# Cross attention and feed-forward on one core: output bias prepared early on 32 rows, weight splits in eight pieces

## The chip, the cores and the metric

One core of one Trainium2 chip runs the kernel in one launch. The metric is the time of an execution on the device in microseconds; several runs are made and their median is compared.

## The reference

x has 16 x 100 = 1600 tokens of 512, the context 16 x 361 = 5776 keys of 512. Sixteen heads of 32 dimensions attend from all tokens to all keys; queries, keys, values and probabilities are rounded to 8 bits. A feed-forward part with 1408 hidden channels follows.

```python
q = (x @ Wq + bq) ; k, v = split(cond @ Wkv + bkv)        # x is layernormed
q, k, v = fq_sym(q * scale), fq_sym(k), fq_sym(v)          # 127 steps, by row / by channel
attn = fq_unsigned(softmax(q @ k.T))                       # 255 steps
x = x + (attn @ v) @ Wp + bp
x13 = quant(layernorm(x)) @ w13.T ; x1, x3 = split(x13)
x = x + quant(rmsnorm(relu(x1) ** 2 * x3) * norm_w) @ w2.T
```

## The kernel before

**Stages.** The program is written out engine by engine, each with its own instruction list and semaphores. First comes *group 0*: keys and values of heads 0 to 3 are computed from 46 blocks of 128 keys (a block is a *unit*, the last has 16 keys; four units are a *batch*, so 12 batches), and between batches the queries of a token tile. For each unit TensorE does four f32 products for the keys (L580), one bf16 product for the key bias (L587) and four f32 products for the values (L582); each f32 product is two passes in the profile. Then comes the main loop over 200 *steps*, `for i in range(NA)`. A step is one tile of 128 tokens of one head against all 5776 keys, in four chunks of 1536 (the last 1168):

- TensorE: scores of the chunk (L640), attention times values of the step four before (L659), and one slice of a unit of the next group (groups 1 to 3) or, from step 160 on, pieces of the output projection (`rows_turn`, `rows_product`).
- VectorE: evicts the chunk from PSUM and takes its minimum (L1120), then the row's minimum (L1142). Between the chunks it takes maxima of the key and value batches.
- ScalarE: one exp over the whole row into bytes (L947), so one L947 a step; it also evicts units.
- SP: issues all transfers in one queue, in order. One transpose of the bytes a step (L524) goes ahead when the exp is done and GpSimd has emptied the buffer (two buffers).
- GpSimd (POOL): unpacks the bytes in four casts a step (`unpack`, L1369), and does key parts, value rounding and the odd jobs. Its order is a list `todo` of (key, work) that is sorted by key; a key is a step with a fraction, and `unpack(i, part)` stands at `i + 2.3 + 0.2 * part`.

Thirteen tiles of the feed-forward part end the program.

**What the change touches.** A bias is added on TensorE as a product of ones with a tile that has the bias in three bf16 parts (high, middle, low), one part in each of rows 0, 1, 2, and zeros below. `BK3` is that tile for the keys; VectorE builds it at the start (s_b3). The product in `unit` contracts over all 128 rows of `ones` and `BK3`. When the last unit is done, the same tile is written again for the output bias (`BP3 = BK3`), by GpSimd in five parts, `bias_parts`, at keys 154.15 to 158.15, from bp that SP loads at step 153 (`BP_AT`) into a buffer of the output rows. `rows_product` reads it (L690) after semaphore r_b3.

`split_w13(k)` splits block k of the feed-forward weight (128 x 2816) into a rounded part and a rest that TensorE reads later. Block 0 is loaded at steps 158 to 161 and split at key 163, block 1 loaded at 177 to 180 and split at key 182. Blocks 2 and 3 are done by other engines at the end.

The two lines that set this order:

```python
todo += [(WP_AT + 8.15 + part, bias_parts, (part,)) for part in range(5)]          # WP_AT = 146
todo += [(step + WSP + 1, split_w13, (k,)) for k, step in EARLY_W.items() if k < 2] # WSP = 4
```

Of the kernel before, what the change touches and what calls it, by code (L numbers as in the profile page):

```python
# [35 lines left out]
ALU = mybir.AluOpType  # L36
# [41 lines left out]
WP_AT = (NG - 1) * PHASE - 4  # L78
BP_AT = WP_AT + 7
EARLY_W = {0: (NG - 1) * PHASE + 8, 1: NA - PAIRT + 2, 2: NA - PAIRT + 10}  # L80
# [3 lines left out]
ROWS_AT = [(NG - 1) * PHASE + 10 + 3 * t for t in range(NT)]  # L84
GSPLIT = 640
W2_SPLIT = [(0, 4), (4, 8), (8, NF)]
RING = 4
# [54 lines left out]
def build(nc, x, ctxt, ctxl, Wq, bq, Wkv, bkv, Wp, bp, w13T, w2T, norm_w, eye, Qd, Kd, Od, Rd, out):  # L142
    ctx = ExitStack()
    with ctx:
# [51 lines left out]
        with ExitStack() as early:  # L196
            BK = tmp("BK", [C], F32, early)
            BR = tmp("BR", [C], F32, early)
            BH = tmp("BH", [C], BF16, early)
            BM = tmp("BM", [C], BF16, early)  # L200
            BL = tmp("BL", [C], BF16, early)
            BQ = tmp("BQ", [C], F32, early)
        S = ring("S", 2, [KP], F32)
        Pr = ring("Pr", 2, [NU // 2, P, 2], U8)
# [16 lines left out]
        with ExitStack() as early:  # L221
# [3 lines left out]
            OT = tmp("OT", [NK - 1, P], F32, early)  # L225
        BP, BPT = XO[0], XO[1].bitcast(BF16)[:, 0:C]
        BP3 = BK3[:, :]
        XIF = [tmp("XIF0", [NK, P], F32R)]
# [33 lines left out]
        def halves(k):  # L262
# [10 lines left out]
                   s_nrm s_nr0 s_un s_ao0 s_ao1 s_dve s_act s_pool   # L273
                   r_ol0 r_ol1 r_x0 r_x1 r_b r_b3 r_tp r_ot r_pr r_xo r_st0 r_st1
                   f_tp f_tpe f_pr f_x1 f_xb0 f_xb1 f_sd1 f_sd1d f_xi f_xit
# [48 lines left out]
        def _(sp):  # L324
# [79 lines left out]
            for g in range(NG):  # L404
                sp.dma_start(BV[:, g:g + 1], bkv[C + g * GC:C + (g + 1) * GC].rearrange("(p a) -> p a", a=1)).then_inc(M["s_bv"], 16)
            load_x(2)
            nxt = RING
            for b in range(NBT):
                if b >= 3:
                    store_k(0, b - 3)  # L410
                while nxt < min(NU, NB * b + 7):
                    load_unit(0, nxt)
                    nxt += 1
                for t in Q_AFTER[b][:1]:
                    if 3 <= t + 3 < NT:
# [71 lines left out]
            for i in range(NA):  # L487
# [15 lines left out]
                if 0 <= i - WP_AT < NK:  # L503
                    k = i - WP_AT
                    sp.dma_start(WP[:, k, :], Wp[k * P:(k + 1) * P, :]).then_inc(M["f_c"], 16)
                if i == BP_AT:
                    sp.wait_ge(M["s_vg"], (NG - 1) * NBT)
                    sp.dma_start(BP, bp.partition_broadcast(P)).then_inc(M["r_b"], 16)
                for k, first in EARLY_W.items():
# [53 lines left out]
        def _(pe):  # L563
            def unit(g, u, slices=range(NK)):
# [12 lines left out]
                for c in slices:  # L577
# [6 lines left out]
                    if c == 1:  # L584
                        if k == 0:
                            pe.wait_ge(M["s_b3"], 1)
                        pe.matmul(bank[0:n, 0:GC], ones[:, 0:n], BK3[:, g * GC:(g + 1) * GC], start=False, stop=True)  # L587
                if NK - 1 in slices:
# [84 lines left out]
            def rows_product(t, piece):  # L673
# [11 lines left out]
                if piece == NK - 1:  # L685
                    if t == 0:
                        pe.wait_ge(M["r_b3"], 1)
                    pe.wait_ge(M[f"r_x{t % 2}"], 16 * (t // 2 + 1))
                pe.matmul(PK[0:n, cols], ident[0:n, 0:n], XR[t % 2][0:n, cols], start=False, stop=False)
                last = pe.matmul(PK[0:n, cols], ones[:, 0:n], BP3[:, cols], start=False, stop=True)  # L690
                if piece == 2 * NK - 1:
# [308 lines left out]
        def _(v):  # L1000
# [262 lines left out]
        def _(gp):  # L1263
# [32 lines left out]
            def v_quant(g, b):  # L1296
# [10 lines left out]
                gp.tensor_scalar(VB[k % VRING][:, 0:w], q, 1.0, -MAGIC, ALU.mult, ALU.add).then_inc(M["s_vg"], 1)  # L1307

            def scale_wp(k):

                gp.wait_ge(M["f_c"], 16 * NK)
                gp.wait_ge(M["s_vr"], NG)
                gp.tensor_scalar(WP[:, k, :], WP[:, k, :], SV[:, k:k + 1], 1.0, ALU.mult, ALU.mult).then_inc(M["s_wp"], 1)

            def bias_parts(part):

                if part == 0:
                    gp.wait_ge(M["r_b"], 16)
                    gp.wait_ge(M["s_ku"], NG * NU)
                    link(gp.tensor_scalar(BP3, BP, 1.0, 0.0, ALU.mult, ALU.add))  # L1320
                    link(gp.tensor_tensor(BP, BP, BP3, ALU.subtract))
                elif part == 1:
                    link(gp.tensor_scalar(BP3, BP3, ident[:, 0:1], 1.0, ALU.mult, ALU.mult))
                    link(gp.tensor_scalar(BPT, BP, 1.0, 0.0, ALU.mult, ALU.add))
                elif part == 2:
                    link(gp.tensor_tensor(BP, BP, BPT, ALU.subtract))
                    link(gp.tensor_scalar(BPT, BPT, ident[:, 1:2], 1.0, ALU.mult, ALU.mult))
                elif part == 3:
                    link(gp.tensor_tensor(BP3, BP3, BPT, ALU.add))
                    link(gp.tensor_scalar(BPT, BP, ident[:, 2:3], 1.0, ALU.mult, ALU.mult))  # L1330
                else:
                    gp.tensor_tensor(BP3, BP3, BPT, ALU.add).then_inc(M["r_b3"], 1)

# [37 lines left out]

            def split_w13(k):

                high, low, full = halves(k)
                gp.wait_ge(M[f"f_w{k % 2}"], 16 * WSP * (k // 2 + 1))
                gp.tensor_scalar(high, full, 1.0, 0.0, ALU.mult, ALU.add).then_inc(M["f_hi"], 1)
                gp.wait_ge(M["f_hi"], k + 1)
                gp.tensor_tensor(low, full, high.bitcast(F32), ALU.subtract).then_inc(M["f_lo"], 1)

            gp.wait_ge(M["cst"], 1)  # L1380
            for b in range(NBT + 1):
                if b < NBT:
                    k_scale(0, b)
                if b:
                    k_parts(0, b - 1)
            for a in range(VRING):
                link(gp.memset(VB[a], 0.0))
# [8 lines left out]
            todo += [(WP_AT + 6.15 + k, scale_wp, (k,)) for k in range(NK)]  # L1396
            todo += [(WP_AT + 8.15 + part, bias_parts, (part,)) for part in range(5)]
            todo += [(i + 2.3 + 0.2 * part, unpack, (i, part)) for i in range(NA) for part in range(NPV)]
            todo += [(PAIRT * (p + 1) + LAG + 1, normalise, (p,)) for p in range(H // 2 - 1)]
            todo += [(step + WSP + 1, split_w13, (k,)) for k, step in EARLY_W.items() if k < 2]  # L1400
            todo += [(NA - PAIRT + FULL + FRONT + LAG + 0.15, normalise_front, ())]
# [59 lines left out]
```

## Time and profile before

| | |
|---|---|
| runs | 1914.78, 1923.21, 1927.03 us; median 1923.21 |
| profiled execution | 1914.62 us, span 1912.7 us |
| TensorE (PE) | 1661.8 us busy, 87% |
| VectorE (DVE) | 1696.9 us busy, 89% |
| ScalarE (ACT) | 1372.0 us busy, 72% |
| GpSimd (POOL) | 1447.2 us busy, 76% |
| group 0 | from the start to about 180 us |
| main loop | from about 175 us to about 1670 us |

The span is the time from the first to the last instruction in the trace; the execution's own time has 1.9 us more around it. The profiled execution is at the low end of the runs. Busy shares are averages over stages with different limits. A wait in brackets behind a row is idle time of that engine just before the row, and what ended it.

### The profile page before, as it was taken

The page shows a single profiled execution, that of the slowest core. Times are in us where ns is not written, and L with a number is a line of the kernel's source. Part 1 is how long each engine was busy: PE and PEld are TensorE (multiplying, and loading weights), DVE is VectorE, ACT ScalarE, POOL GpSimd, SP SyncE. Part 2 cuts the span into 40 slices and gives each one's busy share as a digit, 9 for nine tenths or more (in the row PEclk, how much of TensorE's full clock was granted, in tenths as well). Part 3 has the DMA queues.
Part 4 walks back from the last instruction along what each step waited for, and adds up shares of the span by engine and source line. Part 5 has one row for each costly group of instructions (what it writes and reads, how often), then busy time and mean ns, then how long its engine had stood idle before and what let it go on. Part 6 is the DMA issues. An engine that isn't in the chain of part 4 may idle for free.

```text
span 1912.7 us, 40494 instructions
## 1 busy us (share of the span) xinstructions
PE 1661.8 (87%) x16216; PEld 1129.8 (59%) x16216; DVE 1696.9 (89%) x2665; ACT 1372.0 (72%) x1324; POOL 1447.2 (76%) x1166
## 2 busy tenths in 40 slices
PE   7997888888888888889888888898878888679998
PEld 6884666665556665655556665544445555368876
DVE  6766999999999999999999999999889999976665
ACT  2444888898779898888888888887778878632322
POOL 1341798999998888989988888899988898832332
PEclk9998999997799999977999999755689999889999
DMA  5666989997999899969997998888878988732221
GB/s 177 212 199 172 188 175 179 189 181 144 202 182 189 168 182 185 186 134 202 178 202 152 179 190 167 159 159 148 181 150 165 200 167 158 157 107 51 65 56 45
DMA packets 851482, 309.87 MB, mean 162 GB/s; under 512 B 784928, under 2 KB 813920, under 8 KB 851168
## 3 DMA queue, kind: packets, MB, share of 16 engines
q1 hardware_dynamic: 851296, 307.29, 77.9%
q8 instruction: 129, 2.11, 0.5%
q14 instruction: 57, 0.47, 0.1%
HBM read 74.25 MB, written 39.58 MB: 60 GB/s over the span
## 4 chain that ended last, share of the span: by engine, by line
DVE 36%; PE 23%; POOL 15%; issue 13%; DMA 6%; ACT 5%; SPq 2%; POOLq 0%; DVEq 0%; ACTq 0%
DVE S L1120 32%; POOL PT L1369 11%; PE PS L744 5%; DMA PP<-Pr 4%; PE PS L640 4%; PE PK L580 3%; PE PK L795 3%; PE PS L607 2%; ACT Pr L947 2%; PE PO L659 1%; PE PK L582 1%; POOL VV L1304 1%; PE PO L582 1%; PE PO L580 1%; DVE kam L1034 1%
## 5 line engine op out<-in xcount | busy, mean ns | idle before, releaser
L1120 DVE TENSOR_SCALAR_CACHE_REDUCE S<-PS,SQN 128x1536 f32<-128x1536 f32 (+1 forms) x768 | 1286.8, 1714 | 65.3 <-PE PS L640 56.7
L947 ACT ACTIVATE Pr<-S,MS 128x5888 uint8<-128x5888 f32 x200 | 1041.5, 5207 | 216.1 <-DVE MJ L1142 155.1
L1369 POOL CAST PT<-PP 128x1536 uint16<-128x1536 uint8 (+1 forms) x800 | 1102.4, 1423 | 82.7 <-DMA PP<-Pr 82.0
L640 PE MATMUL PS<-KT,QT 96*128 96x512 bf16 (+1 forms) x2496 | 719.0, 413 | 130.4 <-DVE S L1120 117.9
L659 PEld LDWEIGHTS PO<-VI,PT 128*128 128x128 f16 x9200 | 350.0, 99 | 307.4 <-issue 150.9
L659 PE MATMUL PO<-VI,PT 128*128 128x32 bf16 x9200 | 366.2, 180 | 72.2 <-ACT AO L905 58.7
L640 PEld LDWEIGHTS PS<-KT,QT 96*128 96x128 bf16 (+1 forms) x2496 | 209.0, 104 | 342.4 <-issue 166.6
L580 PE MATMUL PK<-WG,CT 128*128 128x128 f32 (+1 forms) x1272 | 220.6, 303 | 13.1 <-DMA CT<-ctxt 8.1
L582 PE MATMUL PK<-CT,WG 128*128 128x128 f32 (+1 forms) x1272 | 212.7, 295 | 0.0
L580 PEld LDWEIGHTS PK<-WG,CT 128*128 128x128 f32 (+1 forms) x1272 | 172.9, 199 | 16.4 <-issue 11.8
L582 PEld LDWEIGHTS PK<-CT,WG 128*128 128x128 f32 x1272 | 167.0, 194 | 1.8 <-issue 0.6
L744 PE MATMUL PS<-W,XIF 128*128 128x512 f32 (+3 forms) x624 | 144.4, 389 | 10.0 <-issue 6.5
L1272 POOL TENSOR_TENSOR KB<-KB,kam 128x512 f32<-128x512 f32 (+1 forms) x48 | 48.7, 1015 | 130.7 <-DVE kam L1041 130.7
L744 PEld LDWEIGHTS PS<-W,XIF 128*128 128x128 f32 (+1 forms) x624 | 115.1, 190 | 40.0 <-POOL XIF L1412 8.9
L1284 POOL TENSOR_TENSOR KD<-KE,kam 128x512 f32<-128x512 f32 (+1 forms) x48 | 48.6, 1013 | 63.0 <-ACT KE L832 63.0
L819 ACT ACTIVATE KB<-PK 128x128 f32<-128x128 f32 (+1 forms) x159 | 42.8, 269 | 65.5 <-PE PK L582 65.2
L1207 DVE SCALAR_TENSOR_TENSOR G<-PS,sc,TG 128x1408 f32<-128x1408 f32 (+1 forms) x13 | 21.9, 1683 | 58.3 <-PE PS L744 58.3
L992 ACT ACTIVATE TG<-G 128x1408 f32<-128x1408 f32 (+1 forms) x13 | 18.0, 1384 | 77.1 <-DVE G L1207 77.1
L1423 POOL TENSOR_SCALAR GW<-GW,sc 128x1408 f32<-128x1408 f32 (+1 forms) x13 | 18.6, 1434 | 71.2 <-DVE sc L1228 71.2
L795 PE MATMUL PK<-W,IQF 128*128 128x512 f32 (+1 forms) x286 | 68.3, 394 | 4.2 <-POOL IQF L1418 1.8
L1120 DVE DVE_READ_ACCUMULATOR S<-PS,SQN 128x1 f32 x768 | 63.9, 83 | 0.0
L795 PEld LDWEIGHTS PK<-W,IQF 128*128 128x128 f32 (+1 forms) x286 | 51.6, 184 | 19.3 <-issue 5.3
(155 smaller groups left out, 1455.3 us busy)
## 6 DMA issues: line engine op xcount, KB each, us to landing
CT<-ctxt SPq DMA_DIRECT2D x180, 256.0 KB, 3.3
k_rows<-KS SPq DMA_DIRECT2D x44, 512.0 KB, 4.2
q_rows<-QS SPq DMA_DIRECT2D x13, 512.0 KB, 4.2
W13F<-w13T SPq DMA_DIRECT2D x12, 352.0 KB, 3.6
PP<-Pr SPq DMA_TRANSPOSE x200, 5.9
XT<-x SPq DMA_DIRECT2D x12, 256.0 KB, 3.3
XR<-x SPq DMA_DIRECT2D x12, 256.0 KB, 3.3
base_rows<-XO SPq DMA_DIRECT2D x12, 256.0 KB, 3.4
```

The lines of the kernel that those rows point to most:

```text
L580: pe.matmul(bank[0:n, 0:GC], CT[k % RING][:, d, 0:n], WG[:, d, 0, :], start=(d == 0), stop=False)
L582: last = pe.matmul(bank[:, GC:GC + n], WG[:, d, 1, :], CT[k % RING][:, d, 0:n], start=(d == 0), stop=(d == NK - 1))
L640: last = pe.matmul(PS[n % 2][p0:p0 + r, f:f + w], QT[h % 3][0:PARTS * HD, q0:q0 + r], KT[h % 3][0:PARTS * HD, c * CHUNK + f:c * CHUNK + f ...
L659: last = pe.matmul(PO[:, 0:w], PT[i % 2][:, u, :].bitcast(F16), VI[g % 2][:, u, h * HD:h * HD + w], start=(u == 0), stop=(u == NU - 1))
L744: last = pe.matmul(PS[half][0:n, f:f + w], XF[:, c, 0:n], W13[:, c, a, half * FF + f:half * FF + f + w], start=(c == 0 and a == 0), stop=( ...
L795: last = pe.matmul(PK[0:n, :], IQF[t % 2][:, k, 0:n], W2[:, k, a, :], start=(k == 0 and a == 0), stop=(k == NF - 1 and a == WPARTS - 1))
L819: act.activation(KB[kb % 2][0:n, u % NB, :, 0:HD], bank[0:n, 0:GC].rearrange("p (h d) -> p h d", d=HD), ACT.Copy)
L947: act.activation(Pr[i % 2].rearrange("p t q b -> p t b q"), S[i % 2].rearrange("p (t b q) -> p t b q", b=2, q=P), ACT.Exp, bias=MS[:, i % ...
L1120: v.tensor_scalar(S[i % 2][:, c * CHUNK:c * CHUNK + CW[c]], PS[n % 2][:, 0:CW[c]], neg_step, None, ALU.mult, ALU.min, accum_out=MN[:, i % ...
L1272: gp.tensor_tensor(KA, KA, kam[:, kb % 2, 1, 0:m].unsqueeze(2).to_broadcast([P, m, HD]), ALU.mult).then_inc(M["s_kn"], 1)
L1284: gp.tensor_tensor(v3(KD), v3(KE), kam[:, kb % 2, 0, 0:m].unsqueeze(2).to_broadcast([P, m, HD]), ALU.mult).then_inc(M["s_k6"], 1)
L1369: gp.tensor_copy(PT[i % 2][:, 2 * t0:2 * t1, :].rearrange("p (t b) q -> p t b q", b=2), PP[i % 2][:, t0:t1, :].bitcast(U8).rearrange("p t ...
```

## The change

1. `bias_parts` goes. `bias_part(part)` takes bp apart into three bf16 tiles `BPP[0..2]` in full, in batches 2, 3 and 4 of group 0 (two vector operations, two, one). bp is loaded once by SP ahead of the loads of unit 4.
2. In batch 6 of group 0, SP moves one row of each of the three tiles into rows 32, 33, 34 of `BK3`. VectorE waits for these three transfers before the main loop.
3. The key bias products contract over rows 0 to 31 (`KEY_ROWS`), the output bias products over rows 32 to 63 (`OUT_ROWS`).
4. `split_w13(k)` becomes eight pieces of 352 columns, each at a key of its own, one step apart: 163 to 170 and 182 to 189.

```diff
-BP_AT = WP_AT + 7
+WPIECES = 8
+BIAS_AT = 2
+KEY_ROWS, OUT_ROWS = slice(0, 32), slice(32, 64)
...
-        BP, BPT = XO[0], XO[1].bitcast(BF16)[:, 0:C]
-        BP3 = BK3[:, :]
+        BP3 = BK3[OUT_ROWS, :]
...
             load_x(2)
+            sp.dma_start(BP, bp.partition_broadcast(P)).then_inc(M["r_b"], 16)
...
+                if b == BIAS_AT + PARTS + 1:
+                    sp.wait_ge(M["r_bp"], PARTS)
+                    sp.wait_ge(M["s_b3"], 1)
+                    for part in range(PARTS):
+                        row = OUT_ROWS.start + part
+                        sp.dma_start(BK3[row:row + 1, :], BPP[part][row:row + 1, :]).then_inc(M["r_b3"], 16)
...
-                if i == BP_AT:
-                    sp.wait_ge(M["s_vg"], (NG - 1) * NBT)
-                    sp.dma_start(BP, bp.partition_broadcast(P)).then_inc(M["r_b"], 16)
...
-                        pe.matmul(bank[0:n, 0:GC], ones[:, 0:n], BK3[:, g * GC:(g + 1) * GC], start=False, stop=True)
+                        pe.matmul(bank[0:n, 0:GC], ones[KEY_ROWS, 0:n], BK3[KEY_ROWS, g * GC:(g + 1) * GC], start=False, stop=True)
...
-                        pe.wait_ge(M["r_b3"], 1)
+                        pe.wait_ge(M["r_b3"], 16 * PARTS)
...
-                last = pe.matmul(PK[0:n, cols], ones[:, 0:n], BP3[:, cols], start=False, stop=True)
+                last = pe.matmul(PK[0:n, cols], ones[OUT_ROWS, 0:n], BP3[:, cols], start=False, stop=True)
...
+            v.wait_ge(M["r_b3"], 16 * PARTS)
             for i in range(NA):
...
+            def bias_part(part):
+
+                if part == 0:
+                    gp.wait_ge(M["r_b"], 16)
+                gp.tensor_scalar(BPP[part], BP, 1.0, 0.0, ALU.mult, ALU.add).then_inc(M["r_bp"], 1)
+                if part < PARTS - 1:
+                    gp.wait_ge(M["r_bp"], part + 1)
+                    link(gp.tensor_tensor(BP, BP, BPP[part], ALU.subtract))
...
-            def split_w13(k):
-
-                high, low, full = halves(k)
+            def split_w13(k, e):
+
+                cols = slice(e * 2 * FF // WPIECES, (e + 1) * 2 * FF // WPIECES)
+                high, low, full = [half[:, cols] for half in halves(k)]
                 gp.wait_ge(M[f"f_w{k % 2}"], 16 * WSP * (k // 2 + 1))
...
+                if e < WPIECES - 1:
+                    link(gp.tensor_scalar(high, full, 1.0, 0.0, ALU.mult, ALU.add))
+                    link(gp.tensor_tensor(low, full, high.bitcast(F32), ALU.subtract))
+                else:
...
-            todo += [(WP_AT + 8.15 + part, bias_parts, (part,)) for part in range(5)]
...
-            todo += [(step + WSP + 1, split_w13, (k,)) for k, step in EARLY_W.items() if k < 2]
+            todo += [(step + WSP + 1 + e, split_w13, (k, e)) for k, step in EARLY_W.items() if k < 2
+                     for e in range(WPIECES)]
```

GpSimd in the main loop, around keys 154 to 156 of the kernel before. BK is the bias tile, XO a buffer that holds bp there, the CASTs unpack one step.

```order
L1320 TENSOR_SCALAR BK<-XO 128x512 [waits s_ku,r_b]
L1321 TENSOR_TENSOR XO<-XO,BK 128x512 [waits s_pool]
L1369 CAST PT<-PP 128x1536 [waits s_pvp,s_tr0,s_pool]
L1369 CAST PT<-PP 128x1536 [waits s_pvp] x2
L1369 CAST PT<-PP 128x1280 [waits s_pv]
L1344 TENSOR_TENSOR AO<-AO,RZ 128x12x32 [waits s_rz,s_pve]
L1344 TENSOR_TENSOR AO<-AO,RZ 128x12x32 [waits s_pool]
L1347 TENSOR_TENSOR AO<-AO,RZ 128x64 [waits s_pool]
L1313 TENSOR_SCALAR WP<-WP,SV 128x512 [waits s_vr,f_c]
L1323 TENSOR_SCALAR BK<-BK,ident 128x512
L1324 TENSOR_SCALAR XO<-XO 128x512 [waits s_pool]
```

The rows of L1320 to L1332 are gone there. Their successors stand in group 0, between the key parts of one batch and the key scale of the next (line numbers of the changed kernel):

```order
L1301 TENSOR_TENSOR KS<-KE 128x16x32 [waits s_kd,s_k8]
L1321 TENSOR_SCALAR BPP<-BP 128x512 [waits r_b]
L1324 TENSOR_TENSOR BP<-BP,BPP 128x512 [waits r_bp]
L1280 TENSOR_TENSOR KB<-KB,kam 128x16x32 [waits s_kr,s_pool]
L1292 TENSOR_TENSOR KD<-KE,kam 128x512 [waits s_kh,s_kc]
L1295 TENSOR_TENSOR KE<-KD 128x512 [waits s_k6]
L1301 TENSOR_TENSOR KS<-KE 128x16x32 [waits s_kd,s_k8]
L1321 TENSOR_SCALAR BPP<-BP 128x512
L1324 TENSOR_TENSOR BP<-BP,BPP 128x512 [waits r_bp]
```

The nine operations with a wait for the load became five, each pair ahead of a scale that waits for VectorE.

SP's queue in group 0 of the changed kernel, at batch 6:

```order
L366 DMA XT<-x 128x512 [waits s_xn]
L426 DMA BK<-BPP 1x16x32 [waits s_b3,r_bp]
L426 DMA BK<-BPP 1x16x32 x2
L395 DMA q_rows<-QS 128x2048 [waits s_qs]
L341 DMA k_rows<-KS 128x4x512 [waits s_kh,s_kp]
L333 DMA CT<-ctxt 128x512 [waits s_ku] x4
```

The row transfers stand between a load of x and a store of query rows; the loads of the next units (CT) come behind.

GpSimd at the split of block 0, before:

```order
L1376 TENSOR_SCALAR W<-W13F 128x2816 [waits f_w0]
L1378 TENSOR_TENSOR W<-W13F,W 128x2816 [waits f_hi]
L1369 CAST PT<-PP 128x1536 [waits s_pvp,s_tr1]
L1369 CAST PT<-PP 128x1536 [waits s_pvp] x2
L1369 CAST PT<-PP 128x1280 [waits s_pv]
```

and now:

```order
L1376 TENSOR_SCALAR W<-W13F 128x352 [waits f_w0]
L1377 TENSOR_TENSOR W<-W13F,W 128x352 [waits s_pool]
L1367 CAST PT<-PP 128x1536 [waits s_pvp,s_tr1,s_pool]
L1367 CAST PT<-PP 128x1536 [waits s_pvp] x2
L1367 CAST PT<-PP 128x1280 [waits s_pv]
L1376 TENSOR_SCALAR W<-W13F 128x352 [waits f_w0]
L1377 TENSOR_TENSOR W<-W13F,W 128x352 [waits s_pool]
L1367 CAST PT<-PP 128x1536 [waits s_pvp,s_tr0,s_pool]
L1367 CAST PT<-PP 128x1536 [waits s_pvp] x2
L1367 CAST PT<-PP 128x1280 [waits s_pv]
L1376 TENSOR_SCALAR W<-W13F 128x352 [waits f_w0]
```

One long pair became eight short ones with the four casts of a step between each two.

## Rows read from the trace of the kernel before

**Rows 1.** Windows: us, busy us (and instructions) of each engine, TensorE clock, DMA share, GB/s.
```profile
50.00:100.00 50.00, 50.00 (x360) 41.94 (x359) 38.52 (x71) 21.54 (x61) 20.11 (x20) 1.00 0.65 203
```
**Rows 2.** Timeline of ScalarE, the exp of each step: start us, us, idle before.
```profile
1328.95 5.21 ACT L947 ACTIVATE Pr<-S,MS 128x5888 uint8<-128x5888 f32 x1 [1.74 <-DVE MJ L1142]
1335.98 5.21 ACT L947 ACTIVATE Pr<-S,MS 128x5888 uint8<-128x5888 f32 x1 [1.61 <-DVE MJ L1142]
...
1354.05 5.21 ACT L947 ACTIVATE Pr<-S,MS 128x5888 uint8<-128x5888 f32 x1 [4.59 <-DMA PP<-Pr]
...
1382.75 5.21 ACT L947 ACTIVATE Pr<-S,MS 128x5888 uint8<-128x5888 f32 x1 [1.66 <-DVE MJ L1142]
```
**Rows 3.** Timeline of GpSimd at the first part of the bias.
```profile
1328.49 0.70 POOL L1313 TENSOR_SCALAR WP<-WP,SV 128x512 f32<-128x512 f32 x1
1330.72 0.62 POOL L1320 TENSOR_SCALAR BK<-XO 128x512 bf16<-128x512 f32 x1 [1.53 <-DMA XO<-bp]
1331.42 1.16 POOL L1321 TENSOR_TENSOR XO<-XO,BK 128x512 f32<-128x512 f32 x1
1332.64 5.48 POOL L1369 CAST PT<-PP 128x1536 uint16<-128x1536 uint8 x4
```
**Rows 4.** Timeline of GpSimd at the split of block 0.
```profile
1394.08 2.54 POOL L1376 TENSOR_SCALAR W<-W13F 128x2816 fp32r<-128x2816 f32 x1
1396.71 6.18 POOL L1378 TENSOR_TENSOR W<-W13F,W 128x2816 fp32r<-128x2816 f32 x1
1402.84 10.91 POOL L1369 CAST PT<-PP 128x1536 uint16<-128x1536 uint8 x8
```
**Rows 5.** Timeline of ScalarE, exps around the splits of blocks 0 and 1.
```profile
1396.34 5.21 ACT L947 ACTIVATE Pr<-S,MS 128x5888 uint8<-128x5888 f32 x1 [1.04 <-DVE MJ L1142]
...
1415.54 5.21 ACT L947 ACTIVATE Pr<-S,MS 128x5888 uint8<-128x5888 f32 x1 [5.74 <-DMA PP<-Pr]
...
1430.03 5.21 ACT L947 ACTIVATE Pr<-S,MS 128x5888 uint8<-128x5888 f32 x1 [1.66 <-DVE MJ L1142]
...
1443.63 5.21 ACT L947 ACTIVATE Pr<-S,MS 128x5888 uint8<-128x5888 f32 x1 [1.04 <-DVE MJ L1142]
...
1464.53 5.21 ACT L947 ACTIVATE Pr<-S,MS 128x5888 uint8<-128x5888 f32 x1 [1.04 <-DVE MJ L1142]
...
1535.67 5.21 ACT L947 ACTIVATE Pr<-S,MS 128x5888 uint8<-128x5888 f32 x1 [1.66 <-DVE MJ L1142]
...
1572.34 5.21 ACT L947 ACTIVATE Pr<-S,MS 128x5888 uint8<-128x5888 f32 x1 [1.48 <-DVE MJ L1142]
1579.13 5.21 ACT L947 ACTIVATE Pr<-S,MS 128x5888 uint8<-128x5888 f32 x1 [1.42 <-DVE MJ L1142]
```
**Rows 6.** Timeline of GpSimd in group 0.
```profile
72.07 1.05 POOL L1272 TENSOR_TENSOR KB<-KB,kam 128x512 f32<-128x512 f32 x1 [7.16 <-DVE kam L1041]
```
**Rows 7.** Timeline of TensorE, last units of group 0; 128*16 is rows*columns of the array.
```profile
134.53 0.22 PE L587 MATMUL PO<-BK,ones 128*128 128x128 bf16 x1
134.58 1.11 PE L582 MATMUL PO<-CT,WG 128*128 128x128 f32 x8
135.53 1.06 PE L580 MATMUL PK<-WG,CT 128*128 128x128 f32 x8
...
136.48 1.11 PE L582 MATMUL PK<-CT,WG 128*128 128x128 f32 x8
137.52 1.05 PE L580 MATMUL PO<-WG,CT 128*16 128x128 f32 x8
138.40 0.22 PE L587 MATMUL PO<-BK,ones 128*16 128x128 bf16 x1
138.55 1.06 PE L582 MATMUL PO<-CT,WG 128*128 128x16 f32 x8
```
**Rows 8.** Timeline of TensorE, the bias of a unit of group 1 and what follows.
```profile
351.06 0.22 PE L587 MATMUL PK<-BK,ones 128*128 128x128 bf16 x1
351.56 0.82 PE L640 MATMUL PS<-KT,QT 96*128 96x512 bf16 x3 [0.28 <-DVE S L1120]
```

More of the change, by code:

```diff
@@ L202, in build @@
             BQ = tmp("BQ", [C], F32, early)
+            BP = tmp("BP", [C], F32, early)
+            BPP = ring("BPP", PARTS, [C], BF16, early)
         S = ring("S", 2, [KP], F32)
@@ L273, in build @@
                    s_nrm s_nr0 s_un s_ao0 s_ao1 s_dve s_act s_pool
-                   r_ol0 r_ol1 r_x0 r_x1 r_b r_b3 r_tp r_ot r_pr r_xo r_st0 r_st1
+                   r_ol0 r_ol1 r_x0 r_x1 r_b r_bp r_b3 r_tp r_ot r_pr r_xo r_st0 r_st1
                    f_tp f_tpe f_pr f_x1 f_xb0 f_xb1 f_sd1 f_sd1d f_xi f_xit
@@ L1313, in scale_wp @@
                 gp.tensor_scalar(WP[:, k, :], WP[:, k, :], SV[:, k:k + 1], 1.0, ALU.mult, ALU.mult).then_inc(M["s_wp"], 1)
[L1315 to L1332, printed above, removed]
             def normalise(p):
@@ L1370, in unpack @@
                                PP[i % 2][:, t0:t1, :].bitcast(U8).rearrange("p t (q b) -> p t b q", b=2)).then_inc(M["s_un"], 1)
-            def split_w13(k):
-                high, low, full = halves(k)
+            def split_w13(k, e):
+                cols = slice(e * 2 * FF // WPIECES, (e + 1) * 2 * FF // WPIECES)
+                high, low, full = [half[:, cols] for half in halves(k)]
                 gp.wait_ge(M[f"f_w{k % 2}"], 16 * WSP * (k // 2 + 1))
-                gp.tensor_scalar(high, full, 1.0, 0.0, ALU.mult, ALU.add).then_inc(M["f_hi"], 1)
-                gp.wait_ge(M["f_hi"], k + 1)
-                gp.tensor_tensor(low, full, high.bitcast(F32), ALU.subtract).then_inc(M["f_lo"], 1)
+                if e < WPIECES - 1:
+                    link(gp.tensor_scalar(high, full, 1.0, 0.0, ALU.mult, ALU.add))
+                    link(gp.tensor_tensor(low, full, high.bitcast(F32), ALU.subtract))
+                else:
+                    gp.tensor_scalar(high, full, 1.0, 0.0, ALU.mult, ALU.add).then_inc(M["f_hi"], 1)
+                    gp.wait_ge(M["f_hi"], k + 1)
+                    gp.tensor_tensor(low, full, high.bitcast(F32), ALU.subtract).then_inc(M["f_lo"], 1)
             gp.wait_ge(M["cst"], 1)
@@ L1385, in _ @@
                     k_parts(0, b - 1)
+                if 0 <= b - BIAS_AT < PARTS:
+                    bias_part(b - BIAS_AT)
             for a in range(VRING):
```

## The prediction

> **What bounds the kernel now.** I read the page first, then the windows, then the timeline of ScalarE, whose big exp (L947) marks one step of the main loop each time, then GpSimd and TensorE in the stretches that the diff touches. The page shows VectorE and TensorE both busy for over 85% of the span, and its chain of waits gives VectorE's evictions (L1120) the largest share. Three stretches matter here.
>
> The first is group 0, the key and value product ahead of the loop: TensorE is busy 50.00 of 50 us there [rows 1]. What is added to it costs time one for one.
>
> The second is the loop where the bias is taken apart. A step takes 7.03 us when nothing disturbs it (1328.95 to 1335.98), but 1328.95 to 1382.75 holds seven steps in 53.80 us, and the exp at 1354.05 stood 4.59 us for the transpose of an earlier step [rows 2]. That transpose waits until GpSimd has emptied its buffer, and GpSimd was at the bias: 1.53 us of waiting for the transfer of bp, then vector work between the casts [rows 3]. The loss is 53.80 - 7 x 7.03 = 4.6 us.
>
> The third are the two splits of a weight block. GpSimd holds 2.54 + 6.18 us in one piece, 8.76 us from 1394.08 to the next cast at 1402.84 [rows 4]. The exp at 1415.54 then waits 5.74 us for the transpose. 1396.34 to 1430.03 holds four steps in 33.69 us; three steps from 1443.63 to 1464.53 take 20.90, so 6.97 each, and the loss is 33.69 - 27.9 = 5.8 us. For block 1, 1535.67 to 1572.34 holds five steps in 36.67 us; the step behind takes 6.79, so the loss is 36.67 - 33.95 = 2.7 us [rows 5]. Together 13.1 us lie in these three places. Between them the pace is set by VectorE and TensorE, and the change does nothing to that.
>
> **The change part by part.** *Bias out of the loop.* The nine vector operations and the wait go. GpSimd gives up 3.5 us at the first part alone (the bias casts stand between 1328.49 + 0.70 and 1332.64) and has four parts more to do, each ahead of a cast. What is late next is the step itself at 7.03 us. Weight loads of block 0 lie in the same steps and go on lengthening the transposes; I leave 0.4 us for them. Gain 4.2 us, between 2.5 and 4.6.
>
> *Bias ahead of the loop.* Three tensor_scalar of 0.62 and two tensor_tensor of 1.16 us [rows 3] come to 4.2 us, spread over batches 2, 3 and 4 of group 0, where GpSimd stands idle 7.16 us before each key scale [rows 6]. Cost 0. If that cover were gone it would be at most 4.2 us. The load of bp is one more issue on SP ahead of unit 4, and the three row transfers (1 KB each) stand in SP's queue ahead of a store of query rows and the key store; both their waits are met by work done long before. Behind them stand the loads of four units. I take 0; it could be 1 us, if those loads come late. VectorE's new wait ahead of the loop is met more than 50 us earlier. Nothing is queued behind it but the loop that starts later anyway.
>
> *Splits in eight pieces.* A tensor_scalar of 352 columns: 0.62 at 512, 2.54 at 2816, so 0.83 ns a column and 0.49 us. A tensor_tensor: 1.16 and 6.18, 2.18 ns a column, 0.81 us. Gaps behind linked operations are 0.08 and 0.06 us [rows 3, 4]. A piece costs 1.44 us, eight 11.5 instead of 8.8, but a step then asks 5.48 + 1.44 = 6.92 us of GpSimd, once a step. Against 6.97 that fits; I leave 0.6 us of the 5.8 for jitter: gain 5.2, between 2 and 5.8. Against 6.79 it is 0.13 too long for eight steps, 1.0 us, and 0.4 for late transposes: gain 1.3, between -1 and 2.7. The weights are needed only at the end of the loop, so their later finish costs nothing. The three gains are 10.7 us.
>
> *Bias products on 32 rows.* This is the part that the title of the change hardly names. Each of the 184 key bias products (L587) and the 26 output bias products (L690) now contracts over 32 partitions instead of 128, so TensorE goes from a matmul on all rows to one on 32 and back. No row has that shape. The nearest is the last unit of a group, with 16 columns of the array [rows 7]: L582 runs 0.95 us to the next matmul on the full array (134.58 to 135.53), but 1.04 when the next has 16 columns (136.48 to 137.52), and from the bias to L582 it is 0.05 us ordinarily (134.53 to 134.58), 0.15 on the way back to the full array (138.40 to 138.55). So 0.09 in and 0.10 out, 0.19 us per bias product. In group 0 TensorE is the bound and 44 of the 46 units stand on the path (waits stand between the last two and the loop): 44 x 0.19 = 8.4 us. In groups 1 to 3, 138 units would make 26 us if all were exposed, but there TensorE waits 0.28 us for VectorE right behind the bias [rows 8], which covers 0.19; I take 1.1 us. The 26 output products make 4.9 us if exposed; they stand in the loop too, and I take 0.5. Ends of the price: below, -0.05 us, the time that a bias product takes between its neighbours, if on its own rows it ran beside them; above, 0.38, twice what the rows show. I take the value of the rows, the nearest that there are.
>
> The Trainium skill has a rule that speaks against this part: "TensorEngine Tiling", section "Key Properties", says that a change of tiling mode, other than a change of tile, drains the engine. By that rule the trace agrees, with 0.09 and 0.10 us at [rows 7]; the page gives no figure.
>
> **The sum.** -4.2 - 5.2 - 1.3 + 8.4 + 1.1 + 0.5 = -0.7 us. The profiled execution took 1914.62 us (span 1912.7 and 1.9 around it), so 1913.9 for its like. It was at the low end of the runs; their median is 1923.21, 0.45% above. From the median: 1922.5 us. A difference under about 1%, 19 us, can't be told from none on this kernel. So the change should come out as no change: what GpSimd gives back in the loop, TensorE pays in group 0.
>
> **The rivals.**
> *The switch to 32 rows is free.* For it: the matmul that the rows show is narrow in columns, the new ones in rows, and no row has those. Against it: the narrow unit pays on the way in and on the way out, so it looks like a change of shape and not like a cost of the columns. It gives 1923.2 - 10.7 = 1912.5 us. The Trainium skill, "TensorE: Matmul & The Clock Gate", section "Why this matters for your kernels", says that a single matmul over 32 rows takes the same time as one over 128; with that alone this rival's time would hold. The matmul's own duration is the 0.22 us of L587 [rows 7], and it is silent on the changes around it.
>
> *The switch costs more, and the kernel is slower.* Place: group 0, where nothing covers TensorE. Price 0.38 us each, 44 x 0.38 = 16.7, with 1.6 in the rest, against 10.7 gained: +7.6, so 1930.8 us. It decides the sign from (10.7 - 1.6) / 44 = 0.21 us each, and my 0.19 is right below. If the 0.28 of cover in groups 1 to 3 is then too short, 138 times 0.1 us come on top, and that is over 1%, 1944 us.
>
> *The pieces fill GpSimd.* 6.92 us a step leaves no room for late transposes. If both splits lose as much as before, only the bias is gained: -4.2 + 10.0 = +5.8, 1929.0 us. Against it: the loop is double buffered, and a piece goes where GpSimd stood waiting for a transpose.
>
> *The bias gain is hidden anyway*, since the quantised values just before had GpSimd late already: 4.2 us less, 1926.7.
>
> **How the numbers follow.** Forecast 0.48; free switch 0.17; dearer switch 0.20; full GpSimd 0.08; hidden bias gain 0.07. All but the worst of the dearer switch lie within 1% of 1923.2. Faster by over 1% needs 19 us, more than the 13.1 that lie in all three places: 0.03, for what I don't see. Slower by over 1%: 0.08, a third of the dearer switch and a little. Within 1%: 0.89. The range reaches from all 13.1 us gained and no price (1910) to the dearer switch with half the gains lost (+13, 1936), a microsecond wider on each side for the runs' own spread.
>
> **What would show it.** Right: in group 0 the step from bias to L582 at about 0.15 us instead of 0.05, a unit at about 2.09 instead of 1.90 (134.58 to 136.48, [rows 7]), and the first exp of the loop some 8 us later. In the loop no exp waits over 3 us for a transpose near the old 1354 and 1415; GpSimd shows pairs of about 0.5 and 0.8 us between casts. In groups 1 to 3 TensorE's waits for VectorE shrink, and the steps keep their length. Wrong: a unit in group 0 still at 1.90 (free switch) or over 2.2 us (dearer); longer steps in groups 1 to 3; in the split stretches steps of 7.2 us and more with GpSimd never idle.

## The result, and the profile after

The changed kernel takes 1926.08 us (median of 22 runs) where the kernel before takes 1920.90 beside it: ratio 1.0031, interval 1.0016 to 1.0045, so 3 to 9 us slower. A second set of runs gave 1.0039 (1.0017 to 1.0061). The forecast of no change, -0.7 us, was too low: GpSimd's gains came and TensorE and the rest gave back more. The experiments found that one part of the change alone, the splits in pieces, is faster than both kernels: 0.9929 to 0.9955 in three sets of runs. One run of all that follow, of pieces_third, took 2387.88 us at a mean granted clock of 0.552; it is counted among that kernel's 11 runs and left out of every ratio and fit.

The profiled execution of the changed kernel took 1919.13 us. The page, busy time of the engines:

```profile
PE 1686.4 (88%) x16216; PEld 1136.5 (59%) x16216; DVE 1697.6 (89%) x2665; ACT 1373.1 (72%) x1324; POOL 1452.4 (76%) x1190
```

TensorE has the same 16216 instructions as before and is busy 24.6 us longer; VectorE and ScalarE stand within 1.1 us of before, GpSimd has 5.2 us more for its 24 more instructions. The chain of waits, by engine and by line:

```profile
DVE 37%; PE 25%; issue 14%; POOL 10%; DMA 7%; ACT 5%; SPq 3%; POOLq 0%; DVEq 0%; ACTq 0%
DVE S L1128 33%; POOL PT L1367 7%; PE PS L751 5%; PE PS L647 5%; DMA PP<-Pr 4%; PE PK L587 3%; PE PK L802 3%; ACT Pr L954 2%; PE PS L614 2%; PE PK L589 2%; PE PO L666 2%; PE PO L589 1%; PE PK L689 1%; PE PO L587 1%; SPq L531 1%
```

GpSimd has 10% of the chain, 15% before; TensorE 25%, 23% before. Group 0 shows one place where TensorE is busy longer. Timeline of TensorE in the changed kernel, the units that answer to [rows 7]; L594 is the bias product, L589 the values, L587 the keys:

```profile
134.78 0.23 PE L594 MATMUL PO<-BK,ones 32*128 32x128 bf16 x1
134.93 1.16 PE L589 MATMUL PO<-CT,WG 128*128 128x128 f32 x8
135.93 1.06 PE L587 MATMUL PK<-WG,CT 128*128 128x128 f32 x8
136.91 0.22 PE L594 MATMUL PK<-BK,ones 32*128 32x128 bf16 x1
137.07 1.16 PE L589 MATMUL PK<-CT,WG 128*128 128x128 f32 x8
```

The kernel before, between the keys at 135.53 and the values at 136.48 of [rows 7]:

```profile
136.42 0.22 PE L587 MATMUL PK<-BK,ones 128*128 128x128 bf16 x1
```

The product itself takes 0.22 us as before. Around it: 0.15 to the values (0.05 before), 0.98 from the keys to it (0.89 before), and 1.00 over the values (0.95 before). A unit takes 137.07 - 134.93 = 2.14 us instead of 1.90.

Timeline of ScalarE in the changed kernel, exps where the bias was taken apart [rows 2], and at the split of block 0 [rows 5]:

```profile
1355.77 5.21 ACT L954 ACTIVATE Pr<-S,MS 128x5888 uint8<-128x5888 f32 x1 [1.61 <-DVE MJ L1150]
1362.79 5.21 ACT L954 ACTIVATE Pr<-S,MS 128x5888 uint8<-128x5888 f32 x1 [1.61 <-DVE MJ L1150]
1369.80 5.21 ACT L954 ACTIVATE Pr<-S,MS 128x5888 uint8<-128x5888 f32 x1 [1.61 <-DVE MJ L1150]
...
1404.58 5.21 ACT L954 ACTIVATE Pr<-S,MS 128x5888 uint8<-128x5888 f32 x1 [1.03 <-DVE MJ L1150]
1413.12 5.21 ACT L954 ACTIVATE Pr<-S,MS 128x5888 uint8<-128x5888 f32 x1 [1.66 <-DVE MJ L1150]
...
1434.02 5.21 ACT L954 ACTIVATE Pr<-S,MS 128x5888 uint8<-128x5888 f32 x1 [1.66 <-DVE MJ L1150]
```

Both stalls for the transpose, 4.59 and 5.74 us before, are gone: the exps wait for VectorE (MJ) alone. Timeline of GpSimd between two steps there [rows 4]:

```profile
1402.03 0.49 POOL L1376 TENSOR_SCALAR W<-W13F 128x352 fp32r<-128x352 f32 x1
1402.60 0.93 POOL L1377 TENSOR_TENSOR W<-W13F,W 128x352 fp32r<-128x352 f32 x1
1403.59 5.49 POOL L1367 CAST PT<-PP 128x1536 uint16<-128x1536 uint8 x4
1409.06 0.49 POOL L1376 TENSOR_SCALAR W<-W13F 128x352 fp32r<-128x352 f32 x1
```

GpSimd never rests here and takes 7.03 us for a step (1402.03 to 1409.06). Three steps from 1413.12 take 20.90, 6.97 each: the two paces almost meet.

### The profile page after: what moved, and what is told of

The parts are those of the page before. It is cut to its first block, busy times and chain, and to the rows that moved or that the text cites. A ratio compares the mean times of both kernels' runs of the same rounds, so it can differ in the third digit from the quotient of the medians.

```text
span 1917.2 us, 40523 instructions
## 1 busy us (share of the span) xinstructions
PE 1686.4 (88%) x16216; PEld 1136.5 (59%) x16216; DVE 1697.6 (89%) x2665; ACT 1373.1 (72%) x1324; POOL 1452.4 (76%) x1190
## 4 chain that ended last, share of the span: by engine, by line
DVE 37%; PE 25%; issue 14%; POOL 10%; DMA 7%; ACT 5%; SPq 3%; POOLq 0%; DVEq 0%; ACTq 0%
DVE S L1128 33%; POOL PT L1367 7%; PE PS L751 5%; PE PS L647 5%; DMA PP<-Pr 4%; PE PK L587 3%; PE PK L802 3%; ACT Pr L954 2%; PE PS L614 2%; PE PK L589 2%; PE PO L666 2%; PE PO L589 1%; PE PK L689 1%; PE PO L587 1%; SPq L531 1%
## 5 line engine op out<-in xcount | busy, mean ns | idle before, releaser
L647 PEld LDWEIGHTS PS<-KT,QT 96*128 96x128 bf16 (+1 forms) x2496 | 203.7, 104 | 323.7 <-issue 150.8
L587 PE MATMUL PK<-WG,CT 128*128 128x128 f32 (+1 forms) x1272 | 220.2, 303 | 13.3 <-DMA CT<-ctxt 9.0
L589 PE MATMUL PK<-CT,WG 128*128 128x128 f32 (+1 forms) x1272 | 213.4, 295 | 0.0
L587 PEld LDWEIGHTS PK<-WG,CT 128*128 128x128 f32 (+1 forms) x1272 | 172.7, 199 | 16.4 <-issue 12.4
L589 PEld LDWEIGHTS PK<-CT,WG 128*128 128x128 f32 x1272 | 166.2, 193 | 2.8
L689 PE MATMUL PK<-WP,OT 128*128 128x256 f32 (+1 forms) x168 | 62.8, 465 | 0.0
```

The source lines that it names most:

```text
L587: pe.matmul(bank[0:n, 0:GC], CT[k % RING][:, d, 0:n], WG[:, d, 0, :], start=(d == 0), stop=False)
L589: last = pe.matmul(bank[:, GC:GC + n], WG[:, d, 1, :], CT[k % RING][:, d, 0:n], start=(d == 0), stop=(d == NK - 1))
L647: last = pe.matmul(PS[n % 2][p0:p0 + r, f:f + w], QT[h % 3][0:PARTS * HD, q0:q0 + r], KT[h % 3][0:PARTS * HD, c * CHUNK + f:c * CHUNK + f ...
L689: pe.matmul(PK[0:n, cols], OT[:, k, half:half + n], WP[:, k, cols], start=(k == 0 and half == 0), stop=False)
```

## The experiments

There are eighteen measurements: thirteen new kernels, and five repeats. A single profile is a weak witness on this kernel: the kernel before, profiled once more, took 9.9 us longer. So times come from medians, and the profiles serve to read where single steps fall. The ratios are against the kernel before on the same chip; its median in each set is 1918.04, 1919.37, 1921.06, 1917.35 and 1917.94 us.

| kernel | runs | median us | ratio (interval) |
|---|---|---|---|
| narrow_g0 | 6 | 1928.91 | 1.0070 (1.005 to 1.009) |
| narrow_loop | 9 | 1925.51 | 1.0038 (1.0016 to 1.0061) |
| narrow_out | 12 | 1921.18 | 1.0012 (0.9995 to 1.0029) |
| rows96_all | 12 | 1910.06 | 0.9959 (0.9941 to 0.9977) |
| pieces_only | 6 | 1906.29 | 0.9929 (0.9917 to 0.9941) |
| bias_only | 12 | 1921.46 | 1.0006 (0.9986 to 1.0025) |
| rows64, before_again | 1 each | 1936.08, 1924.47 | none: single runs |
| pieces_again | 11 | 1911.21 | 0.9949 (0.9933 to 0.9964) |
| no_bias | 6 | 1907.16 | 0.9937 (0.9916 to 0.9959) |
| early_only | 12 | 1916.20 | 0.9980 (0.9964 to 0.9996) |
| narrow_all | 4 | 1939.01 | 1.0100 (1.0076 to 1.0124) |
| after_again | 12 | 1925.19 | 1.0039 (1.0017 to 1.0061) |
| rows96_again | 12 | 1910.12 | 0.9957 (0.9939 to 0.9976) |
| pieces_rows96 | 8 | 1910.15 | 0.9963 (0.9947 to 0.9979) |
| pieces_third | 11 | 1909.96 | 0.9955 (0.9937 to 0.9974) |
| alloc_only | 8 | 1910.05 | 0.9958 (0.9938 to 0.9979) |
| early_dead | 12 | 1909.81 | 0.9961 (0.9942 to 0.9980) |

Much of the spread between runs of one kernel goes with the mean granted clock of TensorE that each run lists: the correlation is -0.96 over 12 runs of rows96_all, -0.76 over 22 of the changed kernel, and between -0.14 and -0.93 in the other sets of runs of one kernel. I fitted all runs of the five sets together, with a constant for each kernel and each set and one slope for the clock. The slope is -5.8 us for 0.01 more of clock, and the spread (standard deviation) that is left is 3.3 us instead of 4.2. One run of the kernel before has a clock of 0.864, far from all others; without it the slope is -7.8, and the figures below move by 1.1 us at most, each within its own uncertainty. Below, "at equal clock" is a figure of this fit, against the kernel before, with twice its standard error. A change that moved the clock itself would have that part taken out, so the ratios stand beside it.

**The narrow bias products.**

```diff
-pe.matmul(bank[0:n, 0:GC], ones[:, 0:n], BK3[:, g * GC:(g + 1) * GC], ...)
+r = slice(0, 32) if g == 0 else slice(0, P)        # narrow_g0; narrow_loop: if g > 0
+pe.matmul(bank[0:n, 0:GC], ones[r, 0:n], BK3[r, g * GC:(g + 1) * GC], ...)
...
-last = pe.matmul(PK[0:n, cols], ones[:, 0:n], BP3[:, cols], ...)
+last = pe.matmul(PK[0:n, cols], ones[0:32, 0:n], BP3[0:32, cols], ...)   # narrow_out
```

> The kernel before with one edit: the 46 key bias products of group 0 contract over 32 rows, all others over 128 as before. Theory (a change of array shape costs about 0.25 us a bias product, as the changed kernel's units of 2.14 us instead of 1.89 show, and TensorE is the bound in group 0): 44 x 0.25 = 11 us less what a wait of 1.5 us for key context at unit 44 absorbs and what the queries behind it wait anyway, so +7 to +10 us, and the first exp 8 us later. Rival (group 0's loss in the changed kernel came from the load of bp and the row transfers in SP's queue): 0 us.

> The kernel before with one edit: the 138 key bias products of groups 1 to 3 contract over 32 rows. Theory A (TensorE's slack behind a bias does not cover the change of shape in every step: the changed kernel lost 5.0 us between the first exp and step 154, where nothing else was changed): +3 to +7 us. Rival B (the forecast: 0.28 us of slack hides 0.25): 0 to +1 us. Rival C (those 5.0 us are drift between two executions): 0, with the steps' lengths as before.

> The kernel before with one edit: the 26 output bias products contract over 32 rows. Theory (exposed in the third of the steps where the projection runs, since TensorE sets the step there): +2 to +4 us, seen as longer steps every third step from 160 on. Rival (hidden, as forecast): 0 to +0.5 us.

> The kernel before with every bias product, the key's in all four groups and the output's, on 32 rows. The three parts alone measured +13.4, +7.3 and +2.3 us. If the costs add up: +23 us against the kernel before. If they share what the loop can hide: +14 us, which is what the changed kernel is above the same kernel with 96 rows.

At equal clock the four are +12.6 (3.0), +6.3 (2.5), +2.3 (2.3) and, all together, +17.8 (3.5). The first two are clear of zero, the output products alone are not (their ratio's interval is 0.9995 to 1.0029). The parts add up to 21.2, within the uncertainty of 17.8. In groups 1 to 3 the surcharge is visible too. Timeline of TensorE at a unit of narrow_loop, and a like place of before:

```profile
524.92 0.69 PE L580 MATMUL PK<-WG,CT 128*128 128x128 f32 x4
525.55 0.23 PE L588 MATMUL PK<-BK,ones 32*128 32x128 bf16 x1
525.71 0.82 PE L641 MATMUL PS<-KT,QT 96*128 96x512 bf16 x3
```

```profile
506.39 0.69 PE L580 MATMUL PK<-WG,CT 128*128 128x128 f32 x4
506.92 0.22 PE L587 MATMUL PK<-BK,ones 128*128 128x128 bf16 x1
506.98 0.81 PE L640 MATMUL PS<-KT,QT 96*128 96x512 bf16 x3
```

From the keys to the scores it is 0.79 us instead of 0.59: 0.2 more, 138 times, of which 6 us arrive at the end.

**How many rows.** `slice(0, 64)` for all bias products on the kernel before, and on the changed kernel 96 rows for the key, with the output bias in rows 96 to 98 and its products over all 128 rows:

```diff
-KEY_ROWS, OUT_ROWS = slice(0, 32), slice(32, 64)
+KEY_ROWS, OUT_ROWS = slice(0, 96), slice(96, 128)
-last = pe.matmul(PK[0:n, cols], ones[OUT_ROWS, 0:n], BP3[:, cols], ...)
+last = pe.matmul(PK[0:n, cols], oneo[:, 0:n], BP3[:, cols], ...)   # BP3 = BK3[:, :]; oneo: 1 in OUT_ROWS, else 0
```

> The kernel before with key and output bias products over 64 rows. If what is paid is a change of the array's shape, whatever its size, a unit of group 0 takes 2.14 us as with 32 rows. If it grows with the rows left out, about 2.05 us. If only 32 rows are paid for, 1.89 us.

> The changed kernel, but with key bias products over rows 0 to 95, the output bias in rows 96 to 98, and the output bias products over all 128 rows with a stationary tile that is one in rows 96 to 127 and zero above. If the price is that of the array's shape and 96 rows count as the full array (scores have 96 rows), a unit in group 0 is back at 1.89 us and all that GpSimd gives back is kept: -11 to -13 us against the kernel before. Rival (any count of rows other than 128 is paid for): a unit of 2.14 us and +2 to +5 us. Rival (the gain of the pieces is lost elsewhere too): -4 to -8 us.

> The changed kernel with the key products on 96 rows and the output products on 128, once more. Against after_again it has the narrow products taken out and nothing else: 14 to 20 us less (about 0.25 us for each of 211 narrow products, where they are not hidden, is at most 50; group 0 alone is 11).

Timelines of TensorE in group 0, rows64 and then rows96_again:

```profile
133.98 1.16 PE L582 MATMUL PO<-CT,WG 128*128 128x128 f32 x8
134.97 1.06 PE L580 MATMUL PK<-WG,CT 128*128 128x128 f32 x8
135.96 0.23 PE L588 MATMUL PK<-BK,ones 64*128 64x128 bf16 x1
136.12 1.16 PE L582 MATMUL PK<-CT,WG 128*128 128x128 f32 x8
```

```profile
134.51 1.11 PE L590 MATMUL PO<-CT,WG 128*128 128x128 f32 x8
135.46 1.06 PE L588 MATMUL PK<-WG,CT 128*128 128x128 f32 x8
136.35 0.22 PE L595 MATMUL PK<-BK,ones 96*128 96x128 bf16 x1
136.41 1.11 PE L590 MATMUL PK<-CT,WG 128*128 128x128 f32 x8
```

On 64 rows a unit takes 2.14 us as on 32 (133.98 to 136.12), on 96 rows 1.90 as on 128. So the price does not grow with the rows left out: it is there in full at 64 and 32 rows and absent at 96. That 32 and 64 rows make the array change its shape and 96 do not fits this, but is inferred: the rows of the trace name only the rows used (96*128). rows64 is a single execution, of which the unit time is used here. Two sets of runs put the kernel with 96 rows 8 us under before; against after_again it is 14.0 (2.5) us less at equal clock.

> The changed kernel as it is, beside the two runs below on one chip. Its first measurement: ratio 1.0031, some 6 us above the kernel before. The parts alone, added up, give more: narrow products +18 to +20 (narrow_all, narrow_g0 + narrow_loop + narrow_out), the rest of the change -8 (rows96_all), so +10 to +12. If the parts add up, this run should come out nearer 1.005 than 1.003; if they do not, it stays at 1.003 and the splits in pieces take back part of what the narrow products cost.

The changed kernel stayed near its first measurement, +7.4 (2.3) at equal clock. Narrow products 17.8 and the rest -6.6 would make 11; with the uncertainties of both, that can't be told from 7.

**The splits alone, the bias move alone.** pieces_only is the kernel before with `split_w13(k, e)` of the change and nothing else; bias_only is rows96_all with the splits in one piece:

```diff
-            todo += [(step + WSP + 1, split_w13, (k,)) for k, step in EARLY_W.items() if k < 2]
+            todo += [(step + WSP + 1 + e, split_w13, (k, e)) for k, step in EARLY_W.items() if k < 2
+                     for e in range(WPIECES)]
```

> The kernel before with one edit: the two splits in eight pieces each; bias and rows as before. Theory (each split in one piece held GpSimd 8.76 us and cost 5.8 and 2.7 us; the pieces fit the step): -5 to -8 us, no exp near either split waiting over 3 us for a transpose. Rival (6.9 us of GpSimd a step is too much, the loss is spread over eight steps): -2 to +3 us, with steps of 7.2 us and GpSimd never idle.

> The kernel of rows96_all with each split in one piece again, so only the bias is moved, on rows that keep the array's shape. Theory: -3 to -5 us, all of it between steps 154 and 161. Rival (the rounded values just before have GpSimd late anyway, or the early work and the transfers in group 0 cost something): -1 to +2 us. With pieces_only it should add up to rows96_all, -7.9 us.

> The kernel before, unchanged, for a second profile of it. If the 5.0 us that the changed kernel lost between step 0 and step 154 came from its narrow products, this profile has the first one's steps to within 1 us. If they were largely the way that transfers and steps happen to fall, its steps drift from the first one's by several us, above all between steps 42 and 50.

> The kernel before with both splits in eight pieces and nothing else, once more, so that it shares its chip with the two runs beside it. If its first measurement stands (ratio 0.9929), it comes out 12 to 15 us under the kernel before.

The splits in pieces bring -7.3 (1.6) at equal clock over three sets, 9 to 14 us by the ratios. The bias move brings +1.4 (2.4): no gain. Yet its stall is gone. The time between the starts of two exps, counted by steps from the first exp (0), in the twenty profiles:

| steps | what lies there | without the edit | with it |
|---|---|---|---|
| start to 0 | group 0 on 128 or 96 rows; on 32 or 64 | 183.6 to 190.0, mean 186.9 | 194.4 to 196.9, mean 195.4 |
| 154 to 161 | bias in the loop; not | 52.1 to 56.0 | 48.5 to 49.7 |
| 163 to 167 | block 0 in one piece; in eight | 30.8 to 33.7 | 27.2 to 29.5 |
| 181 to 190 | block 1 in one piece; in eight | 65.7 to 69.2 | 61.2 to 64.5 |

No row overlaps. The means differ by +8.5, -5.4, -4.2 and -4.5 us. TensorE's granted clock is not alike in all of them: for block 0 the two profiles of 27.2 us had 1.00. Among profiles with 0.85 to 0.89 it is 32.0 to 33.6 us in one piece and 28.1 to 29.5 in eight, so the gain is not the clock's.

**Where the bias gain goes.** no_bias is pieces_only without any output bias (no load, no operations, and the output products add what the key bias tile holds). early_only is pieces_only with the early bias work of the change on 96 rows added, and the old work kept:

```diff
 # early_only, against pieces_only
+            sp.dma_start(BP, bp.partition_broadcast(P)).then_inc(M["r_b"], 16)    # ahead of unit 4
+                    bias_part(b - BIAS_AT)                                        # GpSimd, group 0
+                        sp.dma_start(BK3[row:row + 1, :], BPP[part][row:row + 1, :]).then_inc(M["r_b3"], 16)
+            v.wait_ge(M["r_b3"], 16 * PARTS)
+                        pe.matmul(bank[0:n, 0:GC], ones[KEY_ROWS, 0:n], BK3[KEY_ROWS, g * GC:(g + 1) * GC], ...)
```

> Splits in eight pieces, and the output bias left out altogether: neither its load nor GpSimd's nine operations run, and the output products read the key bias tile as it stands (the output bias isn't added). It bounds from above what moving the output bias out of the loop can give. Theory A (the move gives 4 us in the loop, and something ahead of the loop or later takes it back): 4 us under pieces_again. Theory B (the stall of the bias steps is made good further on in any case, since the wait behind it is shorter by what it was late): within 1.5 us of pieces_again.

> Splits in eight pieces, the bias work of the changed kernel ahead of the loop (load, GpSimd's parts, three transfers of a row each, key products on 96 rows, VectorE's wait for the rows), and the old bias work in the loop kept as well. It differs from pieces_again by the early work alone. Theory A (the early work costs what the move gives): 4 to 6 us above pieces_again. Theory B (the early work is free, as forecast): within 1.5 us of it.

Theory A (the move gains in the loop, and something else takes it back) has the better of it: against pieces_only and its repeats at equal clock, no_bias is -4.1 (3.1), as the stall of the loop, and early_only is +3.5 (2.5). Both are only just clear of zero. What of the early work costs it?

```diff
 # pieces_rows96, against pieces_only
+                        pe.matmul(bank[0:n, 0:GC], ones[0:96, 0:n], BK3[0:96, g * GC:(g + 1) * GC], ...)
 # alloc_only: tiles for BP, BPP and oneo set aside, unused
+            BE = tmp("BE", [C], F32, early)
+            BPP = ring("BPP", PARTS, [C], BF16, early)
 # early_dead: alloc_only, and
+            sp.dma_start(BE, bp.partition_broadcast(P)).then_inc(M["r_e"], 16)
+                    bias_part(b - BIAS_AT)
```

> Splits in eight pieces and the key bias products on 96 rows instead of 128, no other part of the change. It tells what of the early bias work cost early_only its 5 us against pieces_again. If 96 rows cost something that the unit time of group 0 does not show: 3 to 5 us above pieces_again's ratio of 0.9949 (0.997). If the cost is in the early load, GpSimd's parts, the row transfers or VectorE's wait: 0.993 to 0.995.

> The splits in eight pieces alone, a third time, as the measure for the two runs beside it: 9 to 13 us under the kernel before.

> Splits in eight pieces, and the tiles that the early bias work needs set aside on the chip but not used (one is cleared once ahead of everything), so that what is allocated after them lies elsewhere. If the 4 to 6 us that early_only was above pieces come from where the tiles lie: 4 to 6 us above pieces_third. If from the work itself: within 1.5 us.

> As alloc_only, and the early load of the output bias and GpSimd's five operations of group 0 run, with nobody using them: no row transfers, no wait of VectorE for them, key products on all 128 rows. The old bias work in the loop stays. If load and GpSimd's parts are the cost: 4 to 6 us above alloc_only. If it is the row transfers, the wait or the 96 rows: within 1.5 us of alloc_only.

alloc_only and early_dead stand at 0.9958 and 0.9961 beside pieces_third's 0.9955; at equal clock they are -0.7 (2.8) and +1.6 (2.5) against all three sets of pieces. So no cost of the tiles' place, of the load or of GpSimd's operations was found. The 96 rows are +1.2 (3.1), undecided. What is left is the row transfers, VectorE's wait and the 96 rows together, but early_only is only 1.9 (3.2) above early_dead: that they cost something is not shown either, and I could not part them.

One sign is in the traces. From step 30 to 36 the four profiles that have all three (rows96_all, rows96_again, bias_only, early_only) are 1.3 to 2.7 us longer than before, all others 0.1 at most, the changed kernel's own 0.0. Most of it, 0.9 to 1.9 us, lies between exp 34 and exp 35. That stretch in windows (columns as in [rows 1]), pieces_only and then rows96_again:

```profile
436.56:443.29 6.73, 5.99 (x75) 4.22 (x73) 6.70 (x11) 6.73 (x7) 6.57 (x6) 1.00 1.02 161
```

```profile
439.04:447.06 8.02, 7.65 (x82) 5.57 (x83) 6.36 (x11) 6.96 (x8) 7.86 (x7) 0.79 0.95 135
```

TensorE's granted clock is 0.79 there instead of 1.00. It is 0.79, 0.79, 0.78 and 0.64 in the four and 1.00 in all sixteen others. Timelines of TensorE show the same matmuls at both levels, in pieces_only and rows96_again:

```profile
438.24 0.69 PE L581 MATMUL PK<-WG,CT 128*128 128x128 f32 x4
438.82 0.81 PE L641 MATMUL PS<-KT,QT 96*128 96x512 bf16 x3
```

```profile
441.04 1.18 PE L588 MATMUL PK<-WG,CT 128*128 128x128 f32 x4
442.12 1.49 PE L648 MATMUL PS<-KT,QT 96*128 96x512 bf16 x3
```

So in this stretch the four lose their time while the clock is at the lower of its two levels, 1.2 GHz. Shortly before, TensorE had stood 0.97 us for ScalarE in rows96_all and 1.43 in rows96_again, but 0.97 in alloc_only and early_dead too, where the clock stayed. What makes it fall just there, 200 us after the rows were moved, and whether the early work does, is open.

## Why the prediction was wrong

*Bias products on 32 rows* is the step that failed, by the size of its terms. The mechanism was right: the price is around the product, on the way in (0.09) and out (0.10). Missing was the third place, 0.05 us in the matmuls behind it, so 0.24 us and not 0.19. The narrow matmul taken as the nearest row [rows 7] stood at the end of a group, where the unit behind could not be compared. In group 0 that is 44 x 0.24 = 10.6 for the forecast's 8.4. 8.5 of it reach the first exp, since waits of TensorE further on shrink, above all one for a load of the context, from 1.51 us to 0.48. narrow_g0 measured 12.6 (3.0) to the end; where up to 4 us more arise behind the first exp was not traced. The Trainium skill's rule that the forecast set against this part, "TensorEngine Tiling", section "Key Properties", a change of mode drains the engine, agrees with these rows, which give it its size here, 0.24 us around each product.

The larger miss is in the same step: 1.1 us for groups 1 to 3, because one row showed TensorE waiting 0.28 us for VectorE right behind the bias [rows 8]. Measured are +7.3 us (3.1 to 11.7), 6.3 (2.5) at equal clock. 138 products of 0.2 us make 28; about three quarters were covered, not 95%. One row was taken for 138 places. The output products, 0.5, came to 2.3 (2.3), not clear of the forecast.

*Bias out of the loop*: right where it was read. 4.2 was forecast and 4.6 the most; 5.4 were found in the steps and 4.1 (3.1) in the time of no_bias. *Bias ahead of the loop* was taken as free. For the load and GpSimd's operations no cost was found, +1.6 (2.5) in early_dead, though a tensor_scalar took 1.06 us there, not 0.62. With the row transfers, the wait and 96 rows it came to 3.5 (2.5), which no run took apart. In bias_only the gain and this cost come to +1.4 (2.4) together. Whether the changed kernel with its 32 rows pays the same was not tried apart; it had no fall of the clock at step 34.

*Splits in eight pieces*: block 0 gave 4.2 for 5.2, within its range. Block 1 gave 4.5 for 1.3, beyond its range of 2.7: the profile of before that the loss was read from is the shortest at steps 181 to 190 of all with one-piece splits (65.7 of 65.7 to 69.2). The tensor_tensor of a piece took 0.93 us, not 0.81, and GpSimd was full as the rival feared, at 7.03 us a step against 6.97; the exps kept their 6.97 over the steps shown all the same.

*The sum*, in the forecast's order and with what was found: first exp +8.5, bias stall -5.4, splits -4.2 and -4.5, groups 1 to 3 +6.3, output products +2.3, early work +3.5. That is +6.5 us, beside the measured +5 to +8. The first four come from steps of profiles, the last three from times with 2.3 to 2.5 us of uncertainty each, so that the sum meets the measurement is in part luck. The dearest misses are groups 1 to 3 (5.2), the early work (3.5) and the output products (1.8), 10.5 us together, and all three had been called hidden; the gains in GpSimd came out 3.4 us better than forecast. At 14.1 us they are above the 13.1 that the forecast saw in the three places, which it read from a single profile.

*The rivals*: free switch fell (2.14 us a unit, not 1.90). The dearer switch named the place, and its turning point of 0.21 us a product was passed; its 0.38 was too high, and its 1930.8 us too. Full GpSimd fell with -4.2 and -4.5. Hidden bias gain fell in its place and mechanism, though its 1926.7 us is near the measured time: the gain came and other terms outweighed it.

## What to carry to other kernels

A matmul that needs fewer rows is not cheaper if its neighbours fill the array: count the changes of shape on both sides, in every place, and keep small products in the shape of what surrounds them (zeros in the spare rows, or 96 rows instead of 32). A wait that hides a cost has to be read at many places before it is multiplied by 138. Long work of an engine that feeds a double buffer is worth cutting even where it costs that engine 40% more in all (8 x 1.56 us here instead of 8.76): the pieces alone are as fast as any version found that adds all biases (rows96_all is 0.6 us (2.2) above them at equal clock).

## What the runs showed of the hardware

A bias product on 64 rows between matmuls on 128 rows cost the same 0.24 us a unit as one on 32 (2.14 us instead of 1.90), and one on 96 rows cost nothing (1.90). GpSimd's tensor_scalar of 512 columns took 0.62 us in the main loop [rows 3], and 1.06 in group 0 of the changed kernel:

```profile
68.86 1.06 POOL L1321 TENSOR_SCALAR BPP<-BP 128x512 bf16<-128x512 f32 x1
70.01 1.20 POOL L1324 TENSOR_TENSOR BP<-BP,BPP 128x512 f32<-128x512 f32 x1
```

What slows it there, no run tried. TensorE's granted clock fell for a few microseconds at step 34 in four profiles and in none of the sixteen others, and three score products took 1.49 us there instead of 0.81. Runs of one program on one core spread over 4 to 20 us, part of it along the mean granted clock (0.897 to 0.913 in after_again, 1931.86 and 1913.20 us at the two ends of the clock).
